# Pair-by-pair code for the second phase, and another order of the row gathers on GpSimd

## What is computed

```python
x = x + gnn(layernorm(x), edge_index)          # x: 10000 x 1024, 5000 edges
x = x + ffn(layernorm(x))
# gnn: h = x @ W.T + b; out[src] += d[src] * d[dst] * h[dst] over the edges and one self loop
#      per node, with d = deg ** -0.5 and deg counted over src
# ffn: x @ base_W.T + base_b + (x @ A.T) @ B.T      (shared, rank 16)
#      + sum over the 2 best of 6 experts of gate * (x @ A_e.T) @ B_e.T   (rank 16 each)
```

## Time and profile before

| | |
|---|---|
| median of three runs | 2042.78 us |
| the profiled execution | 2044.74 us, its span 2043.0 us |
| instructions in the span | 31611 |
| TensorE matmul | 1935.7 us busy (95%) |
| VectorE | 1466.5 us (72%) |
| ScalarE | 908.7 us (44%) |
| GpSimd | 937.5 us (46%) |
| granted TensorE clock, mean | 0.987 |
| GpSimd waited for VectorE's `pin` in phase two | 215.7 us, 65 times |
| GpSimd's tick waited for gathers | 149.5 us, 72 times |
| VectorE's scale waited for `pw` | 64.2 us, 77 times |
| VectorE L2170 with no releaser shown ("issue") | 17.0 us, 7 times |

### The profile page before, as it was taken

The page is one execution under the profiler, slowest core; times in us unless marked ns, Lnnn a source line. Parts: engine busy times, 40 slices in busy tenths (PEclk is TensorE's granted clock), DMA queues, the critical chain, the costliest instruction groups (busy, mean ns, idle before and its releaser), DMA issues.

```text
span 2043.0 us, 31611 instructions
## 1 busy us (share of the span) xinstructions
PE 1935.7 (95%) x9583; PEld 1613.6 (79%) x9583; DVE 1466.5 (72%) x3526; ACT 908.7 (44%) x1533; POOL 937.5 (46%) x964
## 2 busy tenths in 40 slices
PE   7999999999999999947999999999999999999999
PEld 6778777777787888836878878788888878888887
DVE  6878888888776777755666767677767767776775
ACT  4455555555555555534333333333334333343342
POOL 1712444444424500146555555555555555555550
PEclk9999999999999999979999999999999999999999
DMA  6524455455444453474323333333333333333321
GB/s 245 213 101 153 163 187 175 160 185 179 160 151 144 148 166 145 155 248 118 82 73 102 105 82 95 91 98 104 103 82 92 102 87 100 103 101 84 94 60 61
DMA packets 148959, 260.20 MB, mean 127 GB/s; under 512 B 56077, under 2 KB 75357, under 8 KB 148822
## 3 DMA queue, kind: packets, MB, share of 16 engines
q1 hardware_dynamic: 99478, 237.85, 33.2%
q0 software_dynamic: 49344, 20.85, 8.0%
HBM read 273.80 MB, written 129.74 MB: 198 GB/s over the span
## 4 chain that ended last, share of the span: by engine, by line
issue 35%; PE 28%; POOL 21%; DVE 10%; ACT 2%; DMA 2%; POOLq 0%; DVEq 0%; SPq 0%; ACTq 0%
POOL acc L863 8%; PE bo L1537 4%; PE bo L1541 4%; PE bo L1539 4%; POOL piece L832 2%; POOL counted L799 2%; PE bo L1397 2%; PE bo L1401 2%; PE bo L1399 2%; POOL xpw L741 2%; POOL pw L948 2%; POOL counts L813 2%; POOL slots L820 2%; DVE acc L2161 2%; POOL tick_pool L716 1%
## 5 line engine op out<-in xcount | busy, mean ns | idle before, releaser
L863 POOL DMA_INDIRECT acc<-h_rows,row_now x312 | 505.5, 1620 | 111.6 <-issue 111.1
L1397 PE MATMUL bo<-wr_hi,left_hi 128*128 128x512 f32 x1008 | 400.1, 397 | 4.5 <-ACT bo L1149 3.1
L1401 PE MATMUL bo<-wr_hi,left_lo 128*128 128x512 f32 x1008 | 394.0, 391 | 0.0
L1399 PE MATMUL bo<-wr_lo,left_hi 128*128 128x512 f32 x1008 | 393.4, 390 | 0.0
L741 POOL TENSOR_TENSOR xpw<-xpin,neg_half 128x1 f32<-128x1 f32 x79 | 72.6, 919 | 491.5 <-DVE xpin L1705 491.5
L1537 PE MATMUL bo<-wr_hi,sum_hi 128*128 128x512 f32 x624 | 249.2, 399 | 9.2 <-DVE acc L2161 7.2
L1539 PE MATMUL bo<-wr_lo,sum_hi 128*128 128x512 f32 x624 | 244.5, 392 | 0.0
L1541 PE MATMUL bo<-wr_hi,sum_lo 128*128 128x512 f32 x624 | 244.2, 391 | 0.0
L1397 PEld LDWEIGHTS bo<-wr_hi,left_hi 128*128 128x128 f32 x1008 | 189.8, 188 | 42.6 <-issue 5.7
L1401 PEld LDWEIGHTS bo<-wr_hi,left_lo 128*128 128x128 f32 x1008 | 189.7, 188 | 40.1
L1399 PEld LDWEIGHTS bo<-wr_lo,left_hi 128*128 128x128 f32 x1008 | 190.0, 189 | 37.1
(11 more groups left out here) (231 smaller groups left out, 4275.8 us busy)
## 6 DMA issues: line engine op xcount, KB each, us to landing
xn<-x SPq DMA_DIRECT2D x79, 512.0 KB, 3.9
r_rows<-xn SPq DMA_DIRECT2D x79, 512.0 KB, 2.6
acc<-r_rows SPq DMA_DIRECT2D x79, 512.0 KB, 4.4
out<-acc SPq DMA_DIRECT2D x79, 512.0 KB
h_rows<-hrow SPq DMA_DIRECT2D x144, 256.0 KB, 3.9
acc<-h_rows,row_now POOLq DMA_INDIRECT x312
wr_raw<-w_t SPq DMA_DIRECT2D x16, 256.0 KB, 6.1
piece<-base_t SPq DMA_DIRECT2D x64, 64.0 KB, 2.8
```

What stands on the lines that cost most here:

```text
L863: nc.gpsimd.indirect_dma_start(to[:], None, h_dram, bass.IndirectOffsetOnAxis(ap=at, axis=0), bounds_check=NPAD - 1, oob_is_err=False, com ...
L1397: nc.tensor.matmul(ps, left_hi[n][:, k, :], wr_hi[n][:, k, :], start=False, stop=False, skip_group_check=True)
L1399: nc.tensor.matmul(ps, left_hi[n][:, k, :], wr_lo[n][:, k, :], start=False, stop=False, skip_group_check=True)
L1401: last = nc.tensor.matmul(ps, left_lo[n][:, k, :], wr_hi[n][:, k, :], start=False, stop=(k == 3), skip_group_check=True)
```

## The change

`pipeline` loses its loop, so that all 39 steps are straight code on each of the five engines. GpSimd's step gets another order: power(1, 1), the cast and `rest_in` of pair i+3, (3, 0), (2, 3), (3, 1), power(2, 0), (3, 2). So rounds of two pairs take turns, and round 2 of a pair, which stood at the head of a step, now stands at the end of the step before it; for pair 2 it is issued ahead of step 0. The waits of each round for its predecessor are kept, and the numbers of gathers, ticks, casts and powers are the same.

```diff
-def pipeline(eng, body, last):
-    a = DEEP
-    b = (PAIRS2 - 3) // DEEP * DEEP
-    for i in range(0, a):
-        body(Pair(i // DEEP, i % DEEP))
-    with eng.Fori(a // DEEP, b // DEEP) as k:
-        for q in range(DEEP):
-            body(Pair(k, q))
-    for i in range(b, last + 1):
+def pipeline(body, last):
+    for i in range(last + 1):
         body(Pair(i // DEEP, i % DEEP))
...
+            def round_of(s, a, r, n):
+
+                if r > 0:
+                    added(s, a, r - 1)
+                carry_wait(n)
+                add_pair(s, a, r)
+
+            round_of(z0, 2, 2, 48)
+
             def step(s):
                 c = 22 + 4 * (s.q % 2)
-                if s.has(2):
-                    added(s, 2, 1)
-                    carry_wait(c)
-                    add_pair(s, 2, 2)
                 if s.has(1):
                     power(s.tile(1, 1))
-                if s.has(2):
-                    added(s, 2, 2)
-                    carry_wait(c + 1)
-                    add_pair(s, 2, 3)
                 if s.has(3):
                     if s.filled(1):
                         for t in range(2):
...
                         added(s, 1, 3)
                     slots_of(s, 3)
                     rest_in(s, 3)
-                    carry_wait(c + 2)
-                    add_pair(s, 3, 0)
+                    round_of(s, 3, 0, c)
+                if s.has(2):
+                    round_of(s, 2, 3, c + 1)
+                if s.has(3):
+                    round_of(s, 3, 1, c + 2)
                 if s.has(2):
                     power(s.tile(2, 0))
                 if s.has(3):
-                    added(s, 3, 0)
-                    carry_wait(c + 3)
-                    add_pair(s, 3, 1)
-
-            pipeline(pool, step, PAIRS2 - 2)
+                    round_of(s, 3, 2, c + 3)
+
+            pipeline(step, PAIRS2 - 2)
```

More of the change, by code:

```diff
@@ L704, in _ @@
             load_right(T4)
-            pipeline(sp, step, PAIRS2)
+            pipeline(step, PAIRS2)
             for q in range(DEEP):
@@ L1375, in step @@
                     begin_second2(s.pair(1), s.mod(1, 2))
-            pipeline(act, step, PAIRS2 - 1)
+            pipeline(step, PAIRS2 - 1)
         @block.tensor
@@ L1685, in step @@
                 low(third_bank[q][:], 0, 1)
-            pipeline(pe, step, PAIRS2 - 1)
+            pipeline(step, PAIRS2 - 1)
         @block.vector
@@ L2270, in step @@
                     y_low(s.pair(1), S3, y_raw[S3])
-            pipeline(dve, step, PAIRS2)
+            pipeline(step, PAIRS2)
 def kernel(x, src, dst, L0_gnn_W, L0_gnn_b, L0_ffn_base_W, L0_ffn_base_b, L0_ffn_shared_A,
```

## The result

The changed kernel takes **2011.42 us** (median of four runs, 2008.95 to 2012.92); the kernel before took 2042.44 us beside it (median of four, 2038.26 to 2043.79). The ratio is 0.985, with a 95% interval of 0.9833 to 0.9868. Forecast were 2011.0 us with 2004 to 2031 around it.

What follows compares the result with a forecast made beforehand. TensorE, busy 95%, was taken to bound the kernel at 26.99 us a step. From the profiled 2044.74 us, -18.91 (jumps) and -13.20 (late powers) gave 2012.6, and 2011 for the median, which stands 2 us lower; range 2004 to 2031.

Steps and rivals of the forecast that it cites:

- TensorE's own pace, 26.99: Phase two: TensorE by itself needs 26.99 us a step, loop or not; steps 0 to 38 lose 38.98 us beyond that.
- The jumps, -18.91, by VectorE alone: Phase two's loop: VectorE's gaps at seven jumps back go, 18.91 us gained; the other engines' jumps are counted at nothing.
- Straight code costs nothing on the path: All 39 steps straight: cost taken as 0; the other bound was what the jumps cost, seven times.
- Rival D: Straight code costs what the jumps did, so the loop's removal does nothing: 2029.5 us, chance 0.08.
- The late powers, -13.20: Steps 2 to 8: GpSimd's powers start late behind rounds awaiting landings; the new order ends this, gaining 13.20 us.
- rival C: GpSimd stays late in all steps, as no jump lets it catch up: 2041 to 2088 us, chance 0.06.
- The timeline of the new order: GpSimd's step, timed from power(1, 1)'s start Y: (3, 0) at Y+2.5, power(2, 0) able to start at Y+14.9, variance at Y+15.1.
- the landing of round 0: GpSimd's (3, 0), for which (3, 1) waits: taken to land 5.3 us after its issue, at Y+11.3.
- The landing of (3, 1): GpSimd's wait ahead of (3, 2): landing between 1.93 and 6.46 us, next power(1, 1) by Y+25.6, due at Y+27.0.
- Start-up, 6.87: Steps 0 to 2: the 6.87 us lost there stay, since the early fills keep their places.
- Rival B: (2, 3) lands late behind (3, 0) and VectorE's statistics wait for it: 2058 us, or 2100; chance 0.09.
- Rival E: Power(2, 0) comes 0.2 to 0.5 us beyond its cover in each step: 2018 to 2029 us, chance 0.07.

Runs made afterwards that it cites:

- dve_straight_only: The changed kernel, but all engines except VectorE keep the loop of the kernel before: 2010.84 us, ratio 0.9828 to 0.9892.
- dve_loop_only: The changed kernel, but VectorE alone keeps the loop of the kernel before: 2030.37 us, ratio 0.9926 to 0.9965.
- old_order_dve_loop: The kernel before with all engines straight except VectorE, which keeps its loop; GpSimd's old order kept: 2039.02 us, ratio 0.9983.
- straight_old_order: The kernel before with the loop gone on all engines, GpSimd's old order kept: 2054.07 us, ratio 1.0073.
- after_again: The changed kernel run once more, unchanged, on the same chip as a variant with a reordered prologue: 2011.61 us, ratio 0.9832 to 0.9875.
- no_turns: The changed kernel with round (2, 3) moved back ahead of the cast and (3, 0), so (3, 1) directly follows (3, 0): 2066.82 us, ratio 1.0126.

## Why the prediction was right, point by point

- **TensorE's own pace, 26.99.** Right: 36 steps of 26.99 on the average in after, 26.98 to 27.00 in dve_straight_only. That 26.99 holds both for the inside of the loop and for straight code was read from two pairs of rows, and it was enough.
- **The jumps, -18.91, by VectorE alone.** Right, and shown: taking away VectorE's loop gives all of it, taking away the other four gives nothing. By the runs the seven jumps are worth 19.2 us with the new order. Counting the other engines' jumps at nothing was a guess in the prediction; dve_loop_only is what makes it a finding.
- **Straight code costs nothing on the path.** Right: no gap of VectorE's own in phase two of after. The Trainium skill (Runtime: NRT & Kernel Launch, Instruction fetch mechanics) says that a crossing in straight code is mostly hidden; the trace agrees, with 0 us that VectorE lost in 39 steps. GpSimd has gaps of its own, but has them with its loop as well (last section). Rival D, 2029.5, falls.
- **The late powers, -13.20.** Right in the sum and in the reason. Steps 2 to 8 of after lose nothing. Not all of the 13.20 were waits: before's six waits for the normalised tile are 10.37 us together (1.55, 3.28, 1.29, 0.94, 0.86, 2.45), and each has some 0.2 of restart behind it. The rest, about 1.6 us, is TensorE's clock. At the end of the last wait (2.45 us, to 1180.08) the granted clock fell to 0.50, the 1.2 GHz level, from 1179.9 to 1183.3, and that step took 31.20. In after it doesn't fall between steps 0 and 38. The remark that VectorE's delay at a jump lets GpSimd catch up is shown by old_order_dve_loop. What the prediction didn't have is why GpSimd stays late: it took the landing of 6.46 us as given, where the residual load, requested 1.3 us ahead of the end of that round's issue, is part of it. With a load there the others took 4.1 to 4.9; what made this one longer still is open.
- **The two parts as a sum.** Here the prediction was right for its own case only. It put -18.91 beside -13.20 as if each were to be had alone. The second, alone, gives 12 us; the first, alone, costs 11. Its rival C says as much, and gave 2041 to 2088 for stalls without a jump; straight_old_order shows 2054.
- **The timeline of the new order**, from Y = 1296.22 in step 12. (3, 0) began at Y+1.9 (2.5 forecast), (2, 3) at Y+5.7 (6.4), (3, 1) at Y+9.9 (12.0), and power(2, 0) stood ready 1.74 us before its variance, which came at Y+15.3 (15.1 forecast, with 0.2 to spare). The largest miss is the landing of round 0: at most 3.8 here and 3.9 to 4.6 in the steps where it is waited for, taken as 5.3. The value of 5.3 came from a row of step 2 in the old order, and was on the safe side.
- **The landing of (3, 1), for which (3, 2) waits, bounded by 1.93 and 6.46.** Right: 1313.12 - 1309.84 = 3.3 in step 12, and 2.3 to 4.3 in the steps where the tick waits. The prediction did not look at (3, 2) itself, in whose middle the residual load now goes out. It isn't late, since it has 11 us until (2, 3) needs it.
- **Start-up, 6.87.** 61.30 - 53.98 = 7.32. By its own words the forecast is wrong if the start-up grows. It grew by 0.45 us, but in after_again and in the four kernels with the new order and some loop, steps 0 to 2 took 60.8 to 61.8, so 0.45 is within what one kernel differs from the next. The 1.8 us that the span gained ahead of step 0 were not forecast. Over all traces step 0 begins between 954.3 and 959.5, so they need not come from the change.
- **2011.0 against 2011.42.** That it is so near is partly luck. Between the profiled executions 33.4 us went, where 32.1 were forecast (31.8 of them between steps 0 and 38). The 2 us that were taken off because the profiled execution of before was slower than the median made up for it: in after the two are equal.
- **Rival B**, the short round behind the long one, would have shown in the statistics waiting for gathers; they waited once. The Trainium skill (DMA: Bandwidth & Descriptors, SWDGE vs HWDGE vs iDMA) says that only one queue is allocated for what GpSimd issues; that (2, 3) can't land before (3, 0) was the prediction's own inference from it, and no run here shows the order, only that both are in time. **Rival E** falls with the 1.2 to 1.7 us to spare.

One thing is open. The runs of before spread widely (2031.6 to 2047.6 over 18 in the first set), and those of old_order_dve_loop too (2027.5 to 2045.7), while each of the five kernels at about 2011 us spread over 9 us at most. This fits a GpSimd that catches up at another step in each execution, but no profile of a quick run of before was taken.

## What to carry to other kernels

When an engine shows idle time with no releaser at each turn of a loop, ask whether it is the one that others wait for: here one engine's jumps cost 19 us and the jumps of the other four none, so one engine's loop had to go. Before removing a stall, look at what it lets catch up, since the kernel without the stall and with nothing else changed was slower. On an engine that issues in order, put work that waits for a landing behind work that is due, and set something useful between an issue and the wait for it: the same rounds with one of them moved by one place took 55 us more.

## What the runs showed of the hardware

- **A plain load lengthens the landing of gathers in flight**: 2.4 us (median) with the load behind their issue or thin, 3.4 and 4.3 (medians, up to 6.5) with the two loads of 512 KB requested before its end. With it gone GpSimd caught up. It isn't the only thing that does: in after, round (3, 1) took up to 4.3 us with no residual load requested until 4.9 us or more behind its issue, and why was not tried.
- **A jump back on VectorE**: two gaps, 2.5 and 1.6 us on the average, with a body of four steps (17.5 and 11.1 us in seven places each in dve_loop_only); one gap of 4.5 to 4.7 with a body of eight. TensorE loses 2.7 to 3.0 and 3.2 to 3.4 of them.
- **GpSimd has gaps ahead of some gathers, with a loop and without.** In after there are gaps without a releaser of 2.37 and 2.42 us, 378 us apart, which is 14 steps or 112 gathers, and others of 1.2 us every 189 us, which is 56 gathers. In the timeline of GpSimd:

```profile
1332.85 2.05 POOL L856 DMA_INDIRECT acc<-h_rows,row_now  x1 [2.37 <-issue]
...
1710.72 1.99 POOL L856 DMA_INDIRECT acc<-h_rows,row_now  x1 [2.42 <-issue]
```

The first used up the time to spare: power(2, 0) behind it, at 1338.57, began 0.1 us behind its variance, and nothing was lost. Gaps at an even distance look like a price of straight code, and they are not. In dve_straight_only GpSimd runs its loop, and has them ahead of the same gathers:

```profile
1332.88 1.74 POOL L868 DMA_INDIRECT acc<-h_rows,row_now  x1 [2.48 <-issue]
...
1710.45 1.97 POOL L868 DMA_INDIRECT acc<-h_rows,row_now  x1 [2.34 <-issue]
```

The gaps of 1.2 us stand in before as well, again 56 gathers apart. The larger ones (1.8 to 3.5 us) are in every kernel of the new order but no_turns, and in none of the old one. They go by the number of gathers and by the order, not by the loop; what they are stays open.
